# Latent attention with quarter mean-square products, and a last expert layer run as one chain with its routing inside

## What is computed

```python
def rmsnorm(x, gamma, eps=1e-08):
    n = jnp.linalg.norm(x, axis=-1, keepdims=True) * x.shape[-1] ** (-0.5)
    return x / jnp.maximum(n, eps) * gamma
qn = rmsnorm(q, qn_g) * scale
kn = rmsnorm(k, kn_g)
sim = jnp.einsum('bhid,bhjd->bhij', qn, kn)
attn = jax.nn.softmax(sim)      # over the 512 latent and 77 context keys
```

```python
gates = jax.nn.softmax(xt @ Wg.T, axis=-1)
scores, inds = jax.lax.top_k(gates, 2)
scores = scores / jnp.sum(scores, axis=-1, keepdims=True)
h = silu(xt @ We_gate) * (xt @ We_up);  y_all = h @ We_down     # all 16 experts
y = sum over the two chosen experts of y_all * scores
shared = silu(xt @ Ws_gate.T) * (xt @ Ws_up.T) @ Ws_down.T
y = y + sigmoid(xt @ Wsg.T) * shared
```

## Time and profile before

| | us |
|---|---|
| median of 3 runs | 1818.52 |
| lowest, highest | 1817.52, 1823.54 |
| the profiled execution, its own time | 1816.07 |
| its span (first to last instruction) | 1814.3 |
| PE busy in the span | 1532.8 (84%) |
| DVE, ACT, POOL busy | 891.0, 680.8, 400.1 |
| latent attention, loop of 32 rounds | about 591 to 1184 |
| last layer, from the first product of its layer norm to the end | 1623.96 to 1814.3 |

### The profile page before, as it was taken

How to read it: one execution, slowest core, us unless ns; L and a number is a source line. 1 busy time by engine, 2 the same in 40 slices (tenths; PEclk the granted TensorE clock), 3 DMA queues, 4 the chain that set the end, 5 groups by cost and what they waited for, 6 DMA issues and landing times. The chain is left out here.

```text
span 1814.3 us, 20965 instructions
## 1 busy us (share of the span) xinstructions
PE 1532.8 (84%) x7590; PEld 693.3 (38%) x7590; DVE 891.0 (49%) x1503; ACT 680.8 (38%) x1135; POOL 400.1 (22%) x387
## 2 busy tenths in 40 slices
PE   5877677568846999999999999969999996776997
PEld 2223222458722333333333333336556563223443
DVE  3758464722245566566566656433333335414443
ACT  3354234212243455556455545422222224352111
POOL 1013001245401354354444435400000000010000
PEclk8889688679968899999999999979999998897999
DMA  8300400469030000000000000020000000010000
GB/s 251 137 0 1 108 1 1 169 209 319 30 121 1 1 1 1 1 1 1 1 1 1 1 1 0 1 99 1 0 0 0 0 0 29 1 57 1 0 0 23
DMA packets 29124, 71.20 MB, mean 39 GB/s; under 512 B 5502, under 2 KB 16767, under 8 KB 27775
## 3 DMA queue, kind: packets, MB, share of 16 engines
q1 hardware_dynamic: 24876, 64.81, 10.5%
q0 software_dynamic: 2048, 4.20, 0.9%
q10 hardware_dynamic: 2112, 1.05, 0.2%
HBM read 65.85 MB, written 7.34 MB: 40 GB/s over the span
## 5 line engine op out<-in xcount | busy, mean ns | idle before, releaser
L1761 ACT ACTIVATE a_prob<-a_TP 128x512 f32<-128x512 f32 x256 | 138.9, 595 | 188.1 <-PE a_TP L1584 187.9
L1858 DVE TENSOR_REDUCE a_lat<-a_SP 128x2 f32<-128x1024 f32 x128 | 156.1, 1220 | 52.3 <-PE a_SP L1553 52.3
L1580 PE MATMUL a_TP<-a_qn,a_kn 64*128 64x512 f32 x512 | 148.9, 645 | 3.0 <-ACT a_prob L1761 3.0
L710 DVE TENSOR_TENSOR f_hv<-f_gl,f_VP 128x512 f32<-128x512 f32 (+1 forms) x96 | 65.9, 686 | 163.9 <-ACT f_gl L676 163.9
L2517 POOL TENSOR_TENSOR a_on<-a_osb,a_rden 128x512 f32<-128x512 f32 x9 | 11.4, 1270 | 555.1 <-ACT a_osb L2281 555.1
L676 ACT ACTIVATE f_gl<-f_HP 128x512 f32<-128x512 f32 (+1 forms) x96 | 57.2, 595 | 201.0 <-PE f_VP L658 201.0
L1595 PE MATMUL a_O<-a_prob,a_V 128*64 128x512 f32 x512 | 122.6, 599 | 0.2 <-ACT a_prob L1761 0.2
L645 PEld LDWEIGHTS f_YP<-f_W,f_hv 128*128 128x128 f32 (+1 forms) x768 | 100.6, 192 | 48.1 <-issue 44.6
L656 PE MATMUL f_HP<-xn,f_W 128*128 (+1 forms) x192 | 104.1, 625 | 16.4 <-PEq L560 11.0
L1973 POOL TENSOR_TENSOR a_acc<-a_prob 128x512 f32<-128x512 f32 x64 | 79.6, 1265 | 159.9 <-ACT a_prob L1761 159.9
L2352 DVE TENSOR_REDUCE a_nm<-a_A 128x8 bf16<-128x616 f32 x96 | 76.6, 798 | 68.7 <-PE a_A L2132 68.5
(11 more groups left out here) (409 smaller groups left out, 2784.8 us busy)
## 6 DMA issues: line engine op xcount, KB each, us to landing
ring_w<-in_F_w SPq DMA_DIRECT2D x64, 512.0 KB
f_yg<-expert_rows SPq DMA_DIRECT2D x12, 256.0 KB, 4.4
a_maskT<-in_maskT SPq DMA_DIRECT2D x1, 2304.0 KB
a_biasT<-in_biasT SPq DMA_DIRECT2D x1, 2304.0 KB
f_b<-in_F_b SPq DMA_DIRECT2D x1, 2048.0 KB
a_biasQ<-in_biasQ SPq DMA_DIRECT2D x1, 1848.0 KB
f_W<-in_F_w SPq DMA_DIRECT2D x1, 1536.0 KB
f_W<-in_F_w SPq DMA_DIRECT2D x1, 1408.0 KB
```

What stands on the lines that cost most here:

```text
L1580: nc.tensor.matmul(TP[0:n, h, :], keys(h), qn[half(h), r % 4, :], start=True, stop=False)
L1761: nc.scalar.activation(prob[0:n, 2 * k + h, :], TP[0:n, h, :], ACT.Exp, bias=rowneg[0:n, b:b + 1] if k == 0 else 0.0).then_inc(p_ready, 1)
L1858: nc.vector.tensor_reduce(lat[:, g % 2, 2 * u:2 * u + 2], SP[:, :, :], AX.X, ALU.max, negate=True).then_inc(s_used, 1)
```

## The change

In the latent attention:

- The banks O and DEN become one tile `MS` of two banks. Queries' and keys' mean squares of a round are made together at s = 2 (`means`), as four products of 64 rows x 64 columns. ACT squares the keys in two halves and stores them with the halves exchanged, so that the four products use the four quarters of the array, and in each 64 partitions of PSUM the two row halves write different banks.
- DVE clips both banks in one instruction of 1024 columns, and ACT's logarithm and exponential take 1024 columns too. `norm_k` stands in the same round behind `shift`, `normalise` ahead of the second maxima reduction, and ACT's `denominators` ahead of the second exponential.
- `means` waits for `o_normed`, since it writes O as well, and the first value product (or, in every eighth round, the output projection) waits for `ms_clipped`.

```diff
-                def mean_q(g):
-                    pe.wait_ge(q_squared, g + 1)
-                    nc.tensor.matmul(DEN[:, :], blk[:, :], sq[:, 0, :], start=True, stop=True).then_inc(qs_ready, 1)
-
-                def mean_k(g, bank=None):
-                    pe.wait_ge(k_squared, g + 1)
-                    nc.tensor.matmul((DEN if bank is None else bank)[:, :], blk[:, :], sq[:, 1, :], start=True,
-                                     stop=True).then_inc(ks_ready, 1)
+                def means(g):
+                    pe.wait_ge(q_squared, g + 1)
+                    pe.wait_ge(k_squared, 2 * g + 2)
+                    for h in range(2):
+                        nc.tensor.matmul(MS[half(h), 0, :], ones64[half(h), :], sq[half(h), 0, :], start=True,
+                                         stop=True)
+                        mm = nc.tensor.matmul(MS[half(1 - h), 1, :], ones64[half(h), :], sq[half(h), 1, :],
+                                              start=True, stop=True)
+                    mm.then_inc(ms_ready, 1)
...
                             if r + 3 < R:
                                 if r:
                                     pe.wait_ge(den_log, r)
-                                mean_q(r + 3)
+                                    pe.wait_ge(o_normed, r)
+                                means(r + 3)
                             if p == 0 and b:
+                                if r + 3 < R:
+                                    pe.wait_ge(ms_clipped, r + 4)
                                 output(b - 1, O, range(NP))
                         if s == 3:
                             if p == 0 and b:
                                 pe.wait_ge(x_updated, b)
+                            elif r + 3 < R:
+                                pe.wait_ge(ms_clipped, r + 4)
                             for k in range(3):
                                 values(r, k)
...
-                            if r + 3 < R:
-                                pe.wait_ge(negm_ready, r + 2)
-                                mean_k(r + 3)
...
+                    for h in range(2):
+                        nc.scalar.activation(sq[half(1 - h), 1, :], KP[half(h), :], ACT.Square).then_inc(k_squared, 1)
+
+                def rms(g):
+                    act.wait_ge(ms_clipped, g + 1)
+                    nc.scalar.activation(lnn[:, :, :], clip[:, :, :], ACT.Ln).then_inc(ms_log, 1)
...
+                    nc.scalar.activation(rn[:, :, :], lnn[:, :, :], ACT.Exp, scale=-0.5).then_inc(ms_rms, 1)
...
+                    nc.vector.tensor_scalar(clip[:, :, :], MS[:, :, :], 1.0 / HD, 1e-16, ALU.mult,
+                                            ALU.max).then_inc(ms_clipped, 1)
```

```diff
-    with pe.Fori(0, B) as b:
-        pe.wait_ge(x_updated, b)
...
-        mm = nc.tensor.matmul(BP[:, u % 2, :], pair[:, u, :], wT[:, tokens(b)], start=True,
-                              stop=True)
...
+                for n in range(N):
+                    b, u = divmod(n, U)
+                    if n < 2:
+                        pe.wait_ge(normed, 2 * n + 2)
+                    else:
+                        pe.wait_ge(silued, n - 1)
+                    nc.tensor.matmul(GU[:, 2 * (n % 2), :], Wg[:, u, :], c.xn[:, tokens(b)], start=True,
+                                     stop=True).then_inc(g_ready, 1)
+                    if n >= 2:
+                        pe.wait_ge(up_mult, n - 1)
+                    nc.tensor.matmul(GU[:, 2 * (n % 2) + 1, :], Wu[:, u, :], c.xn[:, tokens(b)], start=True,
+                                     stop=True).then_inc(u_ready, 1)
+                    if n == 0:
+                        turn(0)
+                    if n >= 2:
+                        down(n - 2)
+                    if u < NE:
+                        if n < 2:
+                            pe.wait_ge(logged, n + 3)
+                        else:
+                            pe.wait_ge(gated, n - 1)
+                        pe.wait_ge(pair_made, 1)
+                        pe.wait_ge(wt_copied, b + 1)
+                        nc.tensor.matmul(BP[:, n % 2, :], pairb[:, u, :], wT[:, b, :], start=True,
+                                         stop=True).then_inc(bp_ready, 1)
+                    elif u == NE:
+                        pe.wait_ge(gated, n - 1)
+                        nc.tensor.matmul(BP[:, n % 2, :], wsg[:, :], c.xn[:, tokens(b)], start=True,
+                                         stop=True).then_inc(bp_ready, 1)
+                    if b + 1 < B and u == 2:
+                        route(b + 1)
+                    if b + 1 < B and u == 7:
+                        turn(b + 1)
+                down(N - 2)
+                down(N - 1)
...
+                for b in range(B):
+                    sp.wait_ge(x_updated, b + 1)
+                    sp.dma_start(out[:, tokens(b)], c.xT[:, tokens(b)]).then_inc(stored, 16)
...
-        quad_attention(c, "a3", 3, "L3_Wq", "L3_Wk", "L3_Wv", wo="L3_Wo", rope=True)
-        shared_moe(c, "f3", 7)
+        shared = SharedWeights(c, ctx)
+        quad_attention(c, "a3", 3, "L3_Wq", "L3_Wk", "L3_Wv", wo="L3_Wo", rope=True, more_loads=shared.load)
+        shared_moe(c, "f3", 7, shared, out)
```

413 lines of the change are left out of this document (259 added, 154 removed).

## The result

| | before | after |
|---|---|---|
| median of the runs (us) | 1818.91 (4 runs, 1817.52 to 1823.54) | 1770.97 (4 runs, 1767.37 to 1774.76) |
| profiled execution, its span | 1816.07, 1814.3 | 1774.76, 1773.0 |
| PE busy, share | 1532.8, 84% | 1506.3, 85% |
| mean granted clock | 0.916 | 0.912 |

The kernel became faster: 0.9738 of the time before, 95% interval 0.971 to 0.9766. The median fell by 47.9 us; the forecast was 1771. The four runs of after lie in two pairs, at 1767.4 and at 1774.5 to 1774.8 us, and the median is the mean of the two inner ones; the profiled execution is of the upper pair. The two profiled spans differ by 41.3 us, and where they differ is read from marks that both traces have: the first projection of the latent layer, the first scores of its loop, and VectorE's last update of `xT` in each layer.

A forecast was written before the change was run, and what follows sets the result against it. PE, busy 84% of the span, was taken as the bound, mostly waiting at the last layer's start. 1816.07 - 39.0 (last layer) - 8.0 (latent: -14.8 + 4.4 + 2.4) = 1769.1, plus 2.45 to the median: forecast 1771, range 1752 to 1790.

The forecast's parts named there:

- Last layer: Last layer, from its first product to the span's end: 151.3 us against 190.3, so -39.0 us.
- Latent rounds: Latent loop: key product saved (0.86 us), new wait 0.34, round 18.00 to 17.48 us, -14.8 us over the rounds.
- wait behind `norm_k`: Latent rounds: `norm_k` delays DVE's maxima reduction, so PE waits 0.34 us before its maxima product every round.
- Rival 2: Latent rounds: PE stays last because `norm_k` overlaps more; round 17.14 us, total 1762 us; chance 0.16.
- wait ahead of each output projection: Latent rounds with an output projection: PE waits 1.48 us for `ms_clipped` directly behind the means, three rounds, +4.4 us.
- Rival 3: Latent means: row halves exclude each other in a bank, quarters go two and two; round 18.34 us, total 1798; chance 0.14.
- Rival 5: Latent means: quarter products run one after the other; group 3.64 us, round 20.06, total 1851 us; chance 0.04.
- Ahead of the loop: Three groups before the latent loop: longer clip, logarithm, exponential chain costs +1.0, +1.0 and +0.4, +2.4 us, between 0 and 4.
- first spreading product: Last layer's start: norm, routing and transposes finish so that it runs 20.0 us in, bounds 17 and 24.
- first clock term of +2.0: Last layer's loop: the clock starts low, two products taking 3.75 us instead of 1.7, +2.0 us.
- Rival 4: Last layer: bursts of routing stop PE, three times 3.6 us; total 1782 us; chance 0.06.
- The weights' transfers: Last layer's weight DMAs move to the layer before, behind its own loads in SP's queue: cost nothing.

The follow-up runs named there:

- e3: The kernel after with `norm_k` moved ahead of `shift`, directly behind the queries' scaling on VectorE; 1755.17 us, 0.9653 of before.
- e8: e5 with the three output projections inside the latent loop moved one step later, behind the fourth chunk's scores; 1756.05 us, 0.965 of before.
- e5: e3 with the three groups ahead of the latent loop in halves again, PE waiting for `prep` only behind the first projections; 1760.70 us, 0.968 of before.
- e1: The kernel after with the last layer and its loads as before, so only the latent layer is changed; 1813.16 us, 0.9962 of before.
- e10: The kernel after plus ten unused products where PE was idle, in the gated layer and last attention; 1765.95 us, 0.9748 of before.
- e2: The kernel before with the last layer of after, its weights loaded in the attention ahead; 1775.64 us, 0.976 of before.
- e12b: e8 once more, word for word, run beside e11b on the same chip; 1746.64 us, 0.9631 of before.
- e6: e4 with GpSimd's last pair of additions in each round on 8 columns instead of 512; 1804.45 us, 0.9913 of before.
- e4: The kernel after with two full products for the means instead of four quarters, keys squared in one activation; 1814.37 us, 0.9981 of before.
- e11b: e8 plus the ten unused products of e10 and more in three further idle stretches of the last attention and last layer; 1743.36 us, 0.9606 of before.

## Why the prediction was right

**The sum.** Last layer -39.0 predicted, -40.9 in the profiles; latent layer -8.0 and -6.7. The forecast of 1771 against a median of 1770.97 is closer than the working deserves: no run took 1771, two took 1767.4 and two 1774.5 or more. For the profiled execution it gave 1769.1, and 1774.76 was measured, 5.7 us more: last layer -1.9, latent layer +1.3, stretch ahead of it -2.5, and +8.9 in `f2` and `a3`, which were not foreseen. Within the latent layer, too, two errors cancel: the loop gained 12.8 us and not 10.4, and the groups ahead of it lost 6.1 and not 2.4. That this profiled execution then lies 3.8 us above the median of its runs, and the one before 2.8 below its own, closes the gap by chance.

**Latent rounds.** The means were taken at 1.06 us and took 1.02. The round was taken at 17.48 and is 17.43. The wait behind `norm_k` was taken at 0.34 us and cost 0.33, as e3 showed by taking it away. Of the 2.4 us by which the loop is better than the sum, the rounds explain 1.4 (28 x 0.05); the rest stays open. Rival 2 (17.14, no wait) is what e3 made of the kernel: 17.10. `ms_clipped` fitted ahead of the values, and the wait ahead of each output projection was taken at 1.48 us and is 1.43 (e8 took it away: -4.5 us).

**Rival 3**, the row halves excluding each other in a bank, is out: four quarters of two row halves start within 0.02 us, two in each bank. The Trainium skill, "TensorEngine Tiling (Array Packing)", section "Gotcha 1: PSUM Pressure", says otherwise. "PSUM — Partial Sum Buffer" of the Trainium skill, section "PSUM bank collisions raise a hardware error", quotes that wide rule as well and reports the collision of two row tiles for the same bank and the same quadrant of partitions; the trace agrees with a rule for that case only. Rival 5 is out with it.

**Ahead of the loop** the term was mis-sized: +2.4 us predicted, +6.1 measured, above its bound of 4. The chain clip, logarithm, exponential became longer by 0.53, 0.43 and 0.43 us (1.22, 1.06, 1.06 against 0.69, 0.63, 0.63), as said, and from the means to the next projection are 5.40 and 5.48 us in after, 4.47 and 4.47 before: +0.93 and +1.01, where +1.0 each was predicted. The distances of the groups grew by 2.08 and 2.29 all the same. The rest lies ahead of the means, where PE does the same projections at another clock. The stretch from the second group's first projection to its means, in after and before (columns as for the attention above):

```profile
545.51:550.02 4.51, 4.51 (x8) 2.02 (x9) 1.41 (x2) 2.30 (x4) 1.93 (x3) 0.64 0.00 0
```
```profile
545.98:549.21 3.23, 3.12 (x8) 1.54 (x9) 1.46 (x2) 2.31 (x4) 1.92 (x3) 1.00 0.00 0
```

The granted clock is 0.64 instead of 1.00 and the stretch 1.28 us longer; in the first group it is 0.51 instead of 0.62, and 1.15 us. PE has no idle time in the stretch in after, and the keys' squares end at 549.28, so the wait for both squares, which the change added, is not what costs here; it shows in the third group alone, with 0.35 us. Another 1.6 us are lost between the third means and the first scores, where the mean clock is 0.76 instead of 0.81. What the term left out is thus the clock. Ahead of the second group PE is idle for 3.07 us, before for 1.55, and in e5, with 1.65, the second group is at 1.00 again. The idle time is not the whole rule: the third group is at 1.00 in after behind 3.08 us and at 0.67 in e5 behind 1.66, and in e1 and e10, whose code is that of after there, it is at 0.67 and 0.68 and the whole way takes 61.9 and 61.7 us. e5 gave 3.7 us of the 6.1 back.

**Last layer.** The first spreading product came at 18.4 us, taken at 20.0: the logits of four token tiles take 0.91 us at full clock (1649.31 to the next gate product at 1650.22), where the earlier trace rows at a low clock had 1.85. The unit is 3.09 and not 2.99 us: from the spreading product to the next are 0.31 us, 0.10 above the 0.21 of a bf16 pass; 0.96 from the down product to the spreading one (1652.02 to 1652.98), 0.10 above 0.86; and 0.97 from the gate to the up product, 0.11 above. The changes of tiling were taken at 0.20 for a unit and cost 0.30. These errors cancel in part: -1.6 in the start, -0.9 in each of three routings, +0.1 in each of 32 units; the loop as a whole, the first clock term of +2.0 with it, came out 0.2 us below its sum. Rival 4 did not happen; no routing burst stopped PE. Behind the last update 3.4 us passed, 3.5 were taken.

**The weights' transfers** cost nothing that shows, as said (e1, e2, e3). **`f2` and `a3`** are the term that was missing: they took 2.5 and 6.4 us more. Both go with the granted clock, which is 0.80 in the mean over `a3` at 129.8 us, 0.85 at 125.3 and 0.88 at 123.3. Whether the change brought this about is not shown: e2, with the latent layer as before, has the long `a3`, e3, with nearly all of the change, the short one, and e8 and e12b differ without any edit.

## What to carry to other kernels

Take the cost of a wait from the distance between the starts of two products with and without it, not from the idle column, and put a new step of another engine where that engine already waits: here one step moved by one place was worth 9.9 us in the loop, where the whole change of the latent layer had gained 12.8. A small step of VectorE that GpSimd's work can hold up (a minimum of 8 columns that took 0.2, 0.8, 1.2 or 3.6 us) is priced by what the other engine does at that time, not by its size. When a change is worth less than 10 us of 1800, compare stretches by marks in the traces, and only those that it touches; the whole time also holds what the clock did in the layers ahead and behind. One profile of a layer at a mixed clock is no measure of it: the same code gave 125.3 and 129.8 us.

## What was not expected of the hardware

- VectorE's minimum of 8 columns with both inputs in SBUF took 0.19 us in the last round, where GpSimd was idle, 0.83 in after, 1.15 in e6 and 3.61 in e4, each time until 0.05 us behind the end of an addition of 1.25 us on GpSimd, in e4 of the third in a row.
- The same attention, with the same code and inputs, took 118.2 to 129.8 us by its granted clock (0.50 to 1.00 in steps of 6 us), and 125.3 and 129.8 in two executions of one and the same kernel. With ten unused products of 0.86 us in PE's idle time the first 36 us of it were at full clock; a gain in the whole time is not shown.
- Four fp32 products of 64 rows, 64 columns and 512 wide ran side by side in 1.02 us, with two row halves in one bank at the same time.
- The same code (e8 and e12b) had medians of 1756.05 and 1746.64 us in two sets of runs, the kernel before 1820.14 and 1816.28 beside them.
- A product with 48 rows between full fp32 ones costs 1.05 us from start to start in fp32 and 0.31 in bf16.
- The same three projections ahead of a group's means took 3.23 us at a granted clock of 1.00 and 4.51 at 0.64, where PE had been idle for 1.55 and for 3.07 us.

The fastest version is e11b, 1743.36 us, 0.9606 of before (after: 0.9738); without any unused product it is e8, run again as e12b, 1746.64 us, 0.9631, and the intervals of the two overlap.
